# Scores of a panel's nodes: dot products on GpSimd and VectorE in place of a turned tangent on TensorE

## What is computed

```python
# layer 0
A = alpha * adj + (1 - alpha) * I                      # rows then divided by their sums
x = layernorm(x + relu((A @ x / A.sum(1)) @ W.T + b))
# layer 1
xt = x * artanh(|x|) / |x|                             # the tangent: a factor for each node (|x| clipped below 1 inside artanh)
par = adj   * sigmoid((xt @ w_par[:128])[:, None] + (xt @ w_par[128:])[None, :] + b_par)
chi = adj.T * sigmoid((xt @ w_chi[:128])[:, None] + (xt @ w_chi[128:])[None, :] + b_chi)
s = chi @ xt + par @ xt
x = layernorm(x + proj(expmap0(s)))                    # a factor for each node again
```

## Time and profile before

| | |
|---|---|
| median of 3 runs | 2232.04 us (2229.4 to 2234.08) |
| profiled execution, its own time | 2227.72 us |
| its span | 2225.6 us, granted TensorE clock 0.982 |
| busy: PE, DVE, POOL, ACT | 2031.1, 1940.7, 1337.4, 1323.4 us |
| DMA | 809.89 MB, 364 GB/s on the mean |

### The profile page before, as it was taken

The page is one execution under the profiler, slowest core; times in us unless marked ns, Lnnn a source line. Parts: engine busy times, 40 slices in busy tenths (PEclk is TensorE's granted clock), DMA queues, the critical chain, the costliest instruction groups (busy, mean ns, idle before and its releaser), DMA issues.

```text
span 2225.6 us, 18692 instructions
## 1 busy us (share of the span) xinstructions
PE 2031.1 (91%) x5248; PEld 919.3 (41%) x5248; DVE 1940.7 (87%) x1856; ACT 1323.4 (59%) x1508; POOL 1337.4 (60%) x639
## 2 busy tenths in 40 slices
PE   7999999999989998999999977998888889889896
PEld 3444444444434433444444433343343334334432
DVE  5757788988989898899898989998998998989897
ACT  0001324354364454444444588989889989899996
POOL 0000304435455445643533677999998998999996
PEclk9999999999999999999999978999999999999998
DMA  9978988989989989988988998999989998998984
GB/s 337 358 279 284 388 300 350 383 343 375 379 318 405 377 343 356 373 332 348 387 338 342 412 421 313 423 376 421 421 366 404 421 421 354 417 421 327 421 340 184
DMA packets 126917, 809.89 MB, mean 364 GB/s; under 512 B 14672, under 2 KB 27216, under 8 KB 31072
## 3 DMA queue, kind: packets, MB, share of 16 engines
q1 hardware_dynamic: 111952, 788.58, 87.9%
q10 hardware_dynamic: 14864, 20.13, 2.7%
HBM read 804.39 MB, written 4.26 MB: 363 GB/s over the span
## 4 chain that ended last, share of the span: by engine, by line
PE 42%; POOL 18%; issue 13%; DVE 12%; ACT 11%; DMA 4%; ACTq 1%; DVEq 0%; POOLq 0%; SPq 0%
PE ps L1146 26%; POOL chi L528 13%; PE ps L1218 11%; DVE dsum L914 4%; ACT chi L734 3%; POOL xA L528 3%; DVE ps L1011 3%; ACT ps L751 2%; DMA ring<-in_g_blk 2%; PE ps L1234 1%; DVE keys L1020 1%; DMA xA<-in_x_g 1%; ACT L734 1%; PE ps L1224 1%; POOL acc L537 1%
## 5 line engine op out<-in xcount | busy, mean ns | idle before, releaser
L528 POOL TENSOR_TENSOR chi<-chi,ring 128x1024 f32<-128x1024 f32 x321 | 819.7, 2568 | 659.9 <-ACT chi L734 603.9
L1218 PE MATMUL ps<-keys,xtA 128*128 128x512 f32 x2048 | 978.5, 610 | 135.1 <-DVE keys L1020 99.6
L1146 PE MATMUL ps<-ring,xA 128*128 128x512 f32 x2048 | 918.5, 598 | 39.5 <-DMA ring<-in_g_blk 19.7
L751 ACT ACTIVATE ps<-scores,prcr 128x1024 f32<-128x1024 f32 x472 | 521.8, 1106 | 404.2 <-DVE keys L1020 387.4
L1218 PEld LDWEIGHTS ps<-keys,xtA 128*128 128x128 f32 x2048 | 378.8, 194 | 661.4 <-issue 622.4
L914 DVE TENSOR_TENSOR dsum<-dsum,ring 128x2048 f32<-128x2048 f32 x240 | 594.3, 2476 | 31.7 <-DMA ring<-in_g_blk 25.2
L1146 PEld LDWEIGHTS ps<-ring,xA 128*128 128x128 f32 x2048 | 387.9, 192 | 530.1 <-issue 493.7
L1020 DVE TENSOR_TENSOR keys<-ps,chi 128x1024 f32<-128x1024 f32 x426 | 521.6, 1224 | 86.6 <-issue 33.2
L1011 DVE TENSOR_TENSOR ps<-ps,ring 128x1024 f32<-128x1024 f32 x378 | 462.0, 1222 | 61.7 <-ACT ps L751 59.2
L734 ACT ACTIVATE chi<-scores,prcr 128x1024 f32<-128x1024 f32 x426 | 483.7, 1135 | 13.3 <-DMA scores<-plcl_d 8.4
L528 POOL TENSOR_TENSOR chi<-chi,xA 128x1024 f32<-128x1024 f32 x105 | 247.0, 2372 | 25.5 <-ACT chi L734 25.4
(11 more groups left out here) (115 smaller groups left out, 830.2 us busy)
## 6 DMA issues: line engine op xcount, KB each, us to landing
ring<-in_g_blk SPq DMA_DIRECT2D x460, 1024.0 KB, 9.2
ring<-in_a_cols SPq DMA_DIRECT2D x187, 1024.0 KB, 9.2
xA<-in_a_cols SPq DMA_DIRECT2D x69, 1024.0 KB, 9.9
xA<-in_g_blk SPq DMA_DIRECT2D x32, 1024.0 KB, 11.3
scores<-plcl_d ACTq DMA_DIRECT2D x22, 512.0 KB, 8.1
xA<-in_x_g ACTq DMA_DIRECT2D x64, 64.0 KB, 11.2
yb<-in_xT ACTq DMA_DIRECT2D x8, 512.0 KB, 8.6
out<-yb SPq DMA_DIRECT2D x4, 512.0 KB, 9.6
```

Of the source, the lines that this page charges most:

```text
L528: pool.tensor_tensor(out=chi(n), in0=chi(n), in1=half(t, n), op=ALU.mult).then_inc(m2_ready, 1)
L751: act.activation(dst, scores[:, row, 0, :], ACT.Sigmoid, bias=prcr[:, 2 * jt:2 * jt + 1]).then_inc(p_ready, 1)
L1146: ins = pe.matmul(Y[:, h * BANK:(h + 1) * BANK], xA[:, tile * D:(tile + 1) * D], t[:, tt * BP + h * BANK:tt * BP + (h + 1) * BANK], start= ...
L1218: ins = pe.matmul(outp[:, h * BANK:(h + 1) * BANK], xtA[:, jt * D:(jt + 1) * D], keys(n)[:, h * BANK:(h + 1) * BANK], start=begins, stop=i ...
```

## The change

The turned tangent goes, and with it `turn_tangent`, `copy_turned_tangent`, `column_scores`, `row_biases` and the old `row_scores`. In their place the four scores of a node are dot products of layer 0's result `res` (before the factor) with four weight vectors, and are then multiplied with the node's factor:

- POOL multiplies `res` (128 x 1024, eight nodes to a partition) by one weight vector repeated eight times, into `prods`, which lies in `yb` (`score_product`); four times for each passage, at ticks 11 to 14.
- DVE sums each of the eight groups of 128 (`score_sum`, a TENSOR_REDUCE), at ticks 12 to 15. There is one `prods`, so each product waits for the sum before it (`dots_ready`), and each sum for its product (`prod_ready`).
- POOL multiplies the 32 sums by the factors and adds the biases (`finish_scores`, tick 16).
- PE turns the 2 x 8 row scores by two small transposes (`row_scores`, tick 18), ACT copies 8 x 256 numbers, and two DMAs take them out (`copy_rows`, tick 20).

The squares go into PSUM (`E`) in place of `yb`. With the shorter chain, units may start at tick 18 in place of 22, and at 24 in place of 27 for a panel's own tiles; rows are loaded from tick 22 in place of 25. The planner then puts 158 units among the pairs in place of 154, and the units beside passages 2, 5 and 6 end at tick 9 in place of 13, while passages 3 and 4 have a unit in every tick, as before. The ticks at which `take_out` and the sum behind it fall move too. In passage 7 the four products stand at late units 19, 20, 22 and 23, the sums at 20, 21, 23 and 24, and the third slot in PSUM is used from late unit 33 on in place of 41. Some small tables of layer 1's end shrink to make room.

The diff, cut to its core:

```diff
@@ -42,15 +42,17 @@
- T_TURN, T_XTT, T_PRP, T_PRCR, T_ROWS, T_COPY, T_LOADL) = (0, 0, 1, 2, 4, 6, 7, 8, 9, 10, 11, 12, 13, 14, 15, 16,
-                                                           18, 18, 19, 20, 22, 23, 25)
+ T_SCORE, T_ROWS, T_COPY, T_LOADL) = (0, 0, 1, 2, 4, 6, 7, 8, 9, 10, 11, 12, 13, 14, 15, 16, 16, 18, 20, 22)
+T_MUL, T_SUM = (11, 12, 13, 14), (12, 13, 14, 15)
-T_UNITS = 22
-T_OWN = 27
-LATE_PE = {2: T_DEG, 6: T_LIN, 27: T_TURN, 31: T_PRP, 34: T_ROWS}
-LATE_ACT = {14: T_STD, 17: T_X1, 19: T_SQ, 21: T_NRM, 24: T_LN, 27: T_XT, 32: T_XTT, 39: T_COPY}
-LATE_DVE = {5: T_INV, 10: T_RES, 11: T_STATS, 14: T_RSTD, 21: T_LOGA, 24: T_FAC, 34: T_PRCR}
+T_UNITS = 18
+T_OWN = 24
+LATE_PE = {2: T_DEG, 6: T_LIN, 28: T_ROWS}
+LATE_ACT = {14: T_STD, 17: T_X1, 19: T_SQ, 21: T_NRM, 24: T_LN, 27: T_XT, 31: T_COPY}
+LATE_DVE = {5: T_INV, 10: T_RES, 11: T_STATS, 14: T_RSTD, 20: T_SUM[0], 21: T_SUM[1], 23: T_SUM[2], 24: T_SUM[3]}
+LATE_POOL = {19: T_MUL[0], 20: T_MUL[1], 22: T_MUL[2], 23: T_MUL[3], 26: T_SCORE}
@@ -143,7 +145,7 @@
-SLOT_TWO, SLOT_THREE = LATE0, LATE0 + 41
+SLOT_TWO, SLOT_THREE = LATE0, LATE0 + 33
@@ -300,15 +302,17 @@
-        xTt = yb
-        rows = xTt[0:2, :]
+        prods = yb.rearrange("p (k d) -> p k d", d=D)
+        rows = yb[0:TPP, 0:2 * P]
-        wl = sb("wl", [P, 2])
-        wr = sb("wr", [P, 2])
+        wb = sb("wb", [P, 4, D])
+        dots = sb("dots", [P, 4, TPP])
+        scored = sb("scored", [P, 4 * TPP])
...
@@ -521,6 +524,35 @@
+            def score_product(r, k):
+                pool.wait_ge(x1_ready, r + 1)
+                pool.wait_ge(h_ready, r + 1)
+                if r == 0 and k == 0:
+                    pool.wait_ge(const_in, 16 * N_CONST)
+                if k > 0:
+                    pool.wait_ge(dots_ready, 4 * r + k)
+                pool.tensor_tensor(out=prods, in0=res.rearrange("p (k d) -> p k d", d=D),
+                                   in1=wb[:, k:k + 1, :].to_broadcast([P, TPP, D]), op=ALU.mult).then_inc(prod_ready, 1)
+            def finish_scores(r):
+                pool.wait_ge(dots_ready, 4 * r + 4)
+                pool.wait_ge(fac_ready, r + 1)
+                pool.wait_ge(rowp_ready, r)
+                pool.tensor_tensor(out=scored.rearrange("p (s k) -> p s k", k=TPP), in0=dots[:, :, :],
+                                   in1=s_fac[:, r * TPP:(r + 1) * TPP].unsqueeze(1).to_broadcast([P, 4, TPP]),
+                                   op=ALU.mult).then_inc(scored_ready, 1)
+                pool.wait_ge(scored_ready, r + 1)
+                pool.wait_ge(bpc2_ready, TPP)
+                pool.tensor_tensor(out=prcr[:, r * 2 * TPP:(r + 1) * 2 * TPP].rearrange("p (k s) -> p s k", s=2),
+                                   in0=scored[:, 2 * TPP:4 * TPP].rearrange("p (s k) -> p s k", k=TPP),
+                                   in1=bpc2.rearrange("p (k s) -> p s k", s=2), op=ALU.add).then_inc(prcr_ready, 1)
+            def passage(r, tick):
+                if tick in T_MUL:
+                    score_product(r, T_MUL.index(tick))
+                if tick == T_SCORE:
+                    finish_scores(r)
             def second_product(n):
...
@@ -604,6 +636,8 @@
                     fold(r - 1)
+                if r > 0:
+                    passage(r - 1, q)
                 if g in UNIT_AT:
...
@@ -654,9 +688,9 @@
-                act.wait_ge(h_ready, r + 1)
+                act.wait_ge(res_ready, r + 1)
                 for k in range(TPP):
-                    ins = act.activation(xTt[:, k * D:(k + 1) * D], res[:, k * D:(k + 1) * D], ACT.Square,
+                    ins = act.activation(E[:, k * D:(k + 1) * D], res[:, k * D:(k + 1) * D], ACT.Square,
                                          accum_out=ss[:, k:k + 1])
...
@@ -675,20 +709,18 @@
-            def copy_turned_tangent(r):
-                act.wait_ge(xTp_ready, r + 1)
-                act.wait_ge(ss_ready, r + 1)
-                act.activation(xTt[:, :], E, ACT.Copy).then_inc(xTt_ready, 1)
             def copy_rows(r):
                 act.wait_ge(rowp_ready, r + 1)
-                act.activation(rows.rearrange("a (c p t) -> a c t p", p=P, t=2),
-                               E[0:2, :].rearrange("a (c t p) -> a c t p", p=P, t=2), ACT.Copy).then_inc(rows_ready, 1)
+                act.wait_ge(dots_ready, 4 * r + 4)
+                act.activation(rows.rearrange("a (p t) -> a t p", t=2),
+                               E[0:TPP, 0:2 * P].rearrange("a (t p) -> a t p", t=2), ACT.Copy).then_inc(rows_ready, 1)
                 act.wait_ge(rows_ready, r + 1)
-                act.dma_start(plcl_d[:, r * BP:(r + 1) * BP], rows).then_inc(rows_out, 16)
+                for k in range(2):
+                    act.dma_start(plcl_d[k, r * BP:(r + 1) * BP].rearrange("(c e) -> c e", e=2 * P),
+                                  rows[k * TPP // 2:(k + 1) * TPP // 2, :]).then_inc(rows_out, 16)
             def load_rows(p, b):
-                act.wait_ge(rows_out, 16 * (p + 1))
+                act.wait_ge(rows_out, 32 * (p + 1))
                 for k in range(2):
@@ -974,10 +1004,11 @@
-            def row_biases(r):
-                dve.wait_ge(prp_ready, r + 1)
-                dve.tensor_tensor(out=prcr[:, r * 2 * TPP:(r + 1) * 2 * TPP], in0=E[:, 0:2 * TPP], in1=bpc2[:, :],
-                                  op=ALU.add).then_inc(prcr_ready, 1)
+            def score_sum(r, k):
+                dve.wait_ge(prod_ready, 4 * r + k + 1)
+                dve.wait_ge(scored_ready, r)
+                dve.tensor_reduce(out=dots[:, k, :], in_=prods, axis=mybir.AxisListType.X, op=ALU.add) \
+                    .then_inc(dots_ready, 1)
@@ -1162,25 +1194,12 @@
-            def turn_tangent(r):
-                pe.wait_ge(xt_ready, r + 1)
-                pe.wait_ge(res_ready, r + 1)
-                for k in range(TPP):
-                    at = r * BP + k * D
-                    ins = pe.transpose(E[:, k * P:(k + 1) * P], xtA[:, at:at + D], ident[:, :])
-                ins.then_inc(xTp_ready, 1)
-            def column_scores(r):
-                pe.wait_ge(xTt_ready, r + 1)
-                for k in range(TPP):
-                    ins = pe.matmul(E[:, 2 * k:2 * k + 2], xTt[:, k * P:(k + 1) * P], wr[:, :], start=True, stop=True)
-                ins.then_inc(prp_ready, 1)
             def row_scores(r):
-                pe.wait_ge(prcr_ready, r + 1)
-                for h in range(BP // BANK):
-                    ins = pe.matmul(E[0:2, h * BANK:(h + 1) * BANK], wl[:, :], xTt[:, h * BANK:(h + 1) * BANK],
-                                    start=True, stop=True)
+                pe.wait_ge(scored_ready, r + 1)
+                pe.wait_ge(ss_ready, r + 1)
+                for t in range(2):
+                    ins = pe.transpose(E[0:TPP, t * P:(t + 1) * P], scored[:, t:2 * TPP:2], ident[:, :])
                 ins.then_inc(rowp_ready, 1)
...
```

64 lines of the change are left out of this document (29 added, 35 removed).

## The result

The changed kernel is slower: 2278.24 us (median of 4 runs, 2272.99 to 2279.28) against 2230.72 us for the kernel before (4 runs in turn with it, 2228.0 to 2234.08). I had forecast 2243 and a range up to 2264: the right side, and 35 us too little.

A forecast was written before the change was run, and what follows sets the result against it. PE bounds the pairs, but beside units in passages DVE sets the pace. -8.4 + 12.6 + 0 - 2.8 + 9 = +10.4 us, from 2227.7 to 2238.1; the median lies 4.3 higher, so 2243 us, range 2208 to 2264.

The forecast's parts named there:

- Passage 0: No units at ticks 10 to 17; PE loses turning and old scores, gains small transposes: -4.2 us.
- passage 1: Same claim as for the passage before it: PE's lighter work gains 4.2 us, -8.4 for the two.
- Passages 3 and 4: Units in every tick; chain of sum, product, second product, key, degree sum makes DVE 14.8 us later: +8.6 and +4, together +12.6.
- the `take_out` wait: PE's 6.57 us wait at tick 16 of passage 4 goes, since `take_out` falls to tick 12: -6.6 us.
- my own first section: What bounds the kernel now: in passage 4 DVE sets the pace and PE follows, degree sums 5.7 to 7.3 us apart.
- Passages 2, 5 and 6: Units end at tick 9; PE's lighter work and vanished waits offset waiting for keys and ring refill: 0 each, -7 to +4.
- the rival on the lag at tick 18: Passages 2, 5 and 6: units start when DVE is latest, PE stands, 7 us each: 2264 us; chance 0.15.
- some 10 us behind: Passages 2, 5 and 6: DVE's lag behind PE by tick 17, at 5.9 us a tick against PE's 3.44.
- Units moved: Four more units among the pairs cost PE +6.8, their absence among late units gives -9.6: together -2.8 us.
- Passage 7: Nothing hides the chain among late units; units 20 and 23 cost +4.7 each: +9 us, from +3 to +16.
- At nothing: Counted as zero: weight loads at the start, smaller copies, the split row store on ACT, shared small tables.
- POOL's room hides it: Rival: POOL is half idle among pairs, so PE keeps its gains, passage 7 costs perhaps 7: 2200 us; chance 0.15.

The follow-up runs named there:

- experiment 3: Changed kernel without the four products per passage, sums running over layer 0's result itself: 2223.04 us, 0.9973 of the kernel before.
- experiment 9: Changed kernel without the products, each sum over 8 of 128 elements of layer 0's result: 2201.72 us, 0.9878 of the kernel before.
- experiment 11: Kernel before with one edit, ACT doing `take_out` ahead of its piece of the passage: 2226.91 us, 0.9991 of the kernel before.
- experiment 4: Changed kernel with the old ticks, units from 22, own units from 27, row transposes at 22: 2283.79 us, 1.0244 of the kernel before.
- Experiment 10: Changed kernel with each product replaced by two memsets that write the same tile and read nothing, waits kept: 2244.08 us, 1.0064 of the kernel before.
- Experiments 1: Changed kernel with the two small row-score transposes moved from tick 18 to 20, their copy to 21: 2280.59 us, 1.0229 of the kernel before.
- experiment 8: Changed kernel with POOL's second product ahead of the passage, plus weight vectors loaded behind the node loads: 2264.61 us, 1.0162 of the kernel before.
- (5): Changed kernel with all products kept but waiting for no sum, sums running over layer 0's result: 2264.0 us, 1.0149 of the kernel before.
- experiment 2: Changed kernel with POOL's second product ahead of the passage's new product: 2265.42 us, 1.0158 of the kernel before.

## Why the prediction was wrong

- **Passage 0: right, passage 1: partly.** Panel 1 costs +0.7 with three more unit products among its pairs (3 x 1.71 = 5.1), so the passage gains 4.4, forecast 4.2. Panel 2 costs +0.6 with one more: passage 1 gains only 1.1. The missing 3.1 us are two waits: 2.6 us for loads (1.2 before), and 2.2 us for `yb` at the panel's end (0.6 before). The second is there without products too (experiment 3), where panel 2 costs -1.4.
- **Passages 3 and 4: the mechanism right, the size half.** The steps came to 0.1 us but for one of 11.5, where the degree sum behind the key takes 3.23 in place of 2.28 because POOL's `acc` (L569) runs. The size was short, 25.7 for 12.6, and the term that fails is what PE was to win back. DVE is 13.1 us later in each passage, 26.2 together (29.6 forecast), and nearly all of it is lost. I had taken off 4.2 us twice for PE's lighter work, 6.6 for the `take_out` wait and 2 for ACT, 17 in all. Where DVE sets the pace, as my own first section says of these passages, that relief is worth little: 2.1 us in experiment 9, and 3.6 for the `take_out` wait in experiment 11.
- **Passages 2, 5 and 6: wrong, the step that failed.** "I count -4.2 - 3.3 + 7.5 = 0 each, and -7 to +4 each as the bounds." They cost 24.5 together, outside the bounds. The loss is near what the rival on the lag at tick 18 gave (7 each), but not by its way, the early start of the units (experiment 4). Four things were wrong.

  First, where PE waits. That "without units PE needs nothing of DVE but ring entries", which I said of passages 0 and 1 and kept for the empty ticks here, is false since this change: the transposes at tick 18 need the scores, and the scores the last sum. PE stands 11.7 us there and 30.8 in the three passages.

  Secondly, how late DVE is. I let the degree sum and the product shut each other out, 5.9 us a tick, but left out the argument and the factor: three of their operations take 2.3 us each behind POOL (L988, L989, L997), 6.9 us in passage 5, and each product stands in turn (4.2). My "some 10 us behind" was short even by my own numbers: 7.4 us at tick 10 and four ticks of 5.9 - 3.44 = 2.46 are 17, less what the ticks without a product give back. Measured are 11 to 15.

  Thirdly, the gains: I took off 4.2 and 3.3 us each, 22.5 together. Experiment 9 has the change nearly without its costs, and there the three panels gain 9.4. A part is lost at the panel's end, where PE waits for `yb`: 12.5 us in experiment 9 and 12.7 after the change, for 4.1 before, and 6.6 with the old ticks (experiment 4). So that wait comes in the main with units that start earlier, not with the products.

  Fourthly, I put PE's clock at nothing. PE in the changed kernel, a few ticks before the end of a panel and at the start of the next:

```profile
942.23 5.40 PE L1178 MATMUL ps<-ring,xA 128*128 128x512 f32 x8 [2.45 <-DMA ring<-in_g_blk]
...
972.16 5.37 PE L1178 MATMUL ps<-ring,xA 128*128 128x512 f32 x8 [2.22 <-DVE yb L949]
```

  These are the products of one pair each, which take 3.60 us elsewhere. The granted clock from 942 to 945 us is 0.61 on the mean. Each of the two stands so costs 1.8 us over its length.

  Experiment 10 shows the cause: it is the products' reading. Without it the three panels cost -0.2 together. Experiments 1 and 4 show that neither the place of the transposes nor the start of the units is the cause.
- **Units moved: right** (-12 among the late units for -9.6). **Passage 7: right** (+6.5 for +9, in its range).
- **At nothing, wrongly:** the loads of the weights. Pair 4 starts at 34.3 us in place of 30.1, and panel 0 costs 3.4 in the profile. What that is worth in the median stays open (experiment 8).
- **The sum of the measured pieces:** the change takes away 28 us (experiment 9; the rival "POOL's room hides it" had 2200 for it), the sums put back 21 (3 over 9), the products 55: -28 + 21 + 55 = +48. These are the steps from one kernel to the next, so they add up to the measured loss by construction; each is shown by its own pair of runs. Of the 55, 14 are waits between product and sum (5), and 19 to 34 are operations that shut each other out (10). The two were measured in different ways and overlap, so they aren't a clean split.

The Trainium skill (SBUF — State Buffer, Who interferes with whom) has rules that these runs bear out: a VectorE instruction with two SBUF inputs contends with a GpSimd instruction that reads SBUF, not with one that only writes it. The memsets of 951 ns and the 34 us are in agreement. By the same section a tensor_reduce on trn2 never contends: in experiment 2 the sum of 863.87 lies wholly within POOL's operation of 861.75 (to 866.17) and takes 1.21 us. It also lists tensor_scalar among the operations that can take the shared pair; the 2.32 us on eight elements agree.

## What to carry to other kernels

Idle time of GpSimd was not free to fill: a GpSimd operation that reads SBUF cost VectorE up to its length (2.3 us here), where VectorE's next operation had two SBUF inputs or was a small tensor_scalar. Count such a pair of operations as one after the other. When a step is shortened, list anew what every engine waits for in it: a small operation, such as two transposes of 0.6 us, can carry the wait of a whole chain. Work taken off an engine that follows another is worth little (2.1 us for 17 here), and a wait of TensorE can cost more than its length, because its clock may be lower behind it (1.8 us a pair here). And a ping-pong through a single buffer costs a full round of both engines' queues, so look what stands ahead in each; the order alone was worth 13 us here.

## What was not expected of the hardware

- An operation of DVE on 8 elements takes 0.16 us alone and 2.3 us behind a POOL operation, one after the other: 2.32 and 2.27 in a row behind two operations of POOL. In passage 5 three such operations of the argument and the factor take 6.9 us in place of some 0.5.
- POOL's operations on 32 and 16 elements stand the same way behind a degree sum: 2.23 and 2.29 us, against 0.25 and 0.22 in experiment 10, where no degree sum ran beside them:

```profile
869.56 0.25 POOL L543 TENSOR_TENSOR scored<-dots,fs 128x32 f32<-128x32 f32 x1 [5.12 <-DVE dots L1012]
869.89 0.22 POOL L548 TENSOR_TENSOR prcr<-scored,bpc 128x16 f32<-128x16 f32 x1
```

- The rows look as if the two engines take turns: the length of the product of 1048.71 (4.24 us) fits a start when DVE's degree sum ends, although DVE had its next operation ready (1050.66: eight elements stand for 2.32 us, the product runs). No run tells whether that is a rule of the order of arrival.
